# Bias and token sum of the feed-forward output on GpSimd instead of VectorE

## The reference, cut to what matters

```python
t = t + attention(_ln_t(t), ...)      # linear attention, 6 heads
h = relu(_qlinear(_ln_t(t), W1, b1))  # 96 -> 384
t = t + _qlinear(h, W2, b2)           # 384 -> 96
```

## Time and profile before

| | |
|---|---|
| three runs | 4664.05, 4664.84, 4667.7 us; median 4664.84 |
| the profiled execution | 4665.67 us |
| its span, first to last instruction | 4663.9 us |
| busy share of the span | PE 89%, DVE 77%, POOL 53%, ACT 52% |
| TensorE's granted clock, mean | 0.956 of full speed |
| loop blocks | about 3472 to 4465 us of the span |
| last block | about 4465 to 4664 us |

### The profile page before, as it was taken

One profiled execution on the slowest core, in us unless ns is written; L12 is line 12 of the kernel. 1 busy time (PEld: TensorE's weight loads), 2 busy tenths in 40 slices (PEclk: granted clock), 3 DMA queues, 4 the chain that ended last, 5 costly groups with the idle time before them and its releaser, 6 DMA issues. The chain is left out here.

```text
span 4663.9 us, 44769 instructions
## 1 busy us (share of the span) xinstructions
PE 4156.8 (89%) x13922; PEld 1791.2 (38%) x13922; DVE 3569.4 (77%) x4331; ACT 2405.1 (52%) x3937; POOL 2479.7 (53%) x1991
## 2 busy tenths in 40 slices
PE   7999999999999999999999999863989888988964
PEld 2333333333333333333333333221546555655543
DVE  4999999999999999999999999976015415414345
ACT  5666667666666667666666666632012312312223
POOL 4778877888778877888778877761000000000000
PEclk8999999999999999999999999996999999999976
DMA  3444444444444444444444444433010010000000
GB/s 94 131 131 139 135 143 135 137 136 145 135 135 138 133 145 137 136 136 142 136 134 139 137 138 135 127 115 100 12 42 18 18 43 17 18 15 4 18 1 14
DMA packets 135434, 459.67 MB, mean 99 GB/s; under 512 B 20623, under 2 KB 23122, under 8 KB 133662
## 3 DMA queue, kind: packets, MB, share of 16 engines
q1 hardware_dynamic: 135198, 456.82, 32.0%
HBM read 431.28 MB, written 20.97 MB: 97 GB/s over the span
## 5 line engine op out<-in xcount | busy, mean ns | idle before, releaser
L668 POOL TENSOR_TENSOR prod<-states,c_rows 128x512 f32<-128x512 f32 x1536 | 1935.9, 1274 | 591.5 <-DVE states L600 575.7
L600 DVE TENSOR_TENSOR_SCAN states<-decay,carry,bpsum 128x512 f32<-128x512 f32 x1536 | 1937.6, 1262 | 0.0
L357 PE MATMUL ypsum<-prod,identity 128*128 128x512 f32 x3072 | 1587.8, 598 | 0.4 <-POOL prod L668 0.3
L459 ACT ACTIVATE decay<-delta,decay_rate 128x512 f32<-128x512 f32 x1536 | 1078.4, 716 | 722.3 <-DVE states L600 623.6
L587 DVE TENSOR_TENSOR bpsum<-bpsum,dx 128x512 f32<-128x512 f32 x1536 | 1034.8, 674 | 89.9 <-PE bpsum L350 71.7
L350 PE MATMUL bpsum<-b_rows,select 96*128 96x512 bf16 x1536 | 595.4, 388 | 163.7 <-DVE states L600 162.1
L357 PEld LDWEIGHTS ypsum<-prod,identity 128*128 128x128 f32 x3072 | 592.0, 194 | 311.3 <-issue 176.3
L350 PEld LDWEIGHTS bpsum<-b_rows,select 96*128 96x128 bf16 x1536 | 147.9, 96 | 1068.1 <-DVE states L600 666.2
L1073 PE MATMUL convp<-img_hi,w_hi 96*96 96x512 f16 (+1 forms) x1568 | 483.4, 385 | 65.1 <-PEq L1476 49.0
L1434 DVE SCALAR_TENSOR_TENSOR x<-convp,unscale,x_group 96x1024 f32<-96x1024 f32 x16 | 20.4, 1278 | 406.3 <-PE convp L1073 406.3
L1073 PE MATMUL convp<-img_hi,w_lo 128*96 128x512 f16 (+1 forms) x896 | 276.3, 388 | 0.0
(11 more groups left out here) (215 smaller groups left out, 4526.2 us busy)
## 6 DMA issues: line engine op xcount, KB each, us to landing
c_rows<-c_map SPq DMA_DIRECT2D x512, 512.0 KB, 3.7
c_rows<-c_map SPq DMA_DIRECT2D x512, 256.0 KB, 3.9
x_in<-in_x SPq DMA_DIRECT2D x16, 384.0 KB, 6.0
fused_map<-fused SPq DMA_DIRECT2D x16, 384.0 KB, 5.1
work<-fused_map SPq DMA_DIRECT2D x4, 1536.0 KB, 9.8
x<-in_x SPq DMA_DIRECT2D x4, 1536.0 KB, 16.1
x_biased_map<-work SPq DMA_DIRECT2D x4, 1536.0 KB, 7.1
x_group<-x_biased_map SPq DMA_DIRECT2D x16, 384.0 KB, 3.7
```

What stands on the lines that cost most here:

```text
L357: pe.matmul(ypsum[:, group % Y_BANKS, :], identity[:, :], prod[:, n % P_RING, :], start=s == 0, stop=s == STATES - 1).then_inc(summed, 1)
L459: act.activation(decay[:, n % RING, :], delta[k % 2][:, g, :], ACT.Exp, scale=decay_rate[:, ORDER[k][0], g, s:s + 1]).then_inc(decay_ready, 1)
L600: dve.tensor_tensor_scan(states[:, n % H_RING, :], decay[:, n % RING, :], bpsum[:, n % B_BANKS, :], carry[:, at, u:u + 1], ALU.mult, ALU.a ...
L668: pool.tensor_tensor(prod[:, n % P_RING, :], states[:, n % H_RING, :], c_rows[:, n // C_STATES % C_RING, n % C_STATES, :], ALU.mult).then_ ...
```

## The change

DVE's `mlp` loses `add_bias` and both calls of it. A GpSimd program of its own is added to every block with token work. It issues the same two additions, with the same waits and the same semaphores, for the chunks of both layers in order. No other line changes; nothing is computed otherwise.

```diff
                     def mlp(layer):
-                        def add_bias(c):
-                            dve.wait_ge(t_taken, fill_mlp_o(layer, c) + 1)
-                            y = y16[:, c % 2, :, :]
-                            dve.tensor_tensor(y, y, b2[:, layer, :, :], ALU.add).then_inc(y_biased, 1)
-                            dve.wait_ge(y_biased, CHUNKS * layer + c + 1)
-                            tiles = slice(4 * c, 4 * c + 4)
-                            dve.tensor_tensor(t[:, tiles, :], t[:, tiles, :], y, ALU.add).then_inc(t_step, 1)
...
                             to_fp8(c, THIRDS - 1)
-                            if c > 0:
-                                add_bias(c - 1)
-                        add_bias(CHUNKS - 1)
...
+                if tok:
+                    @block.gpsimd
+                    def _(pool):
+                        for layer in range(2):
+                            for c in range(CHUNKS):
+                                pool.wait_ge(t_taken, fill_mlp_o(layer, c) + 1)
+                                y = y16[:, c % 2, :, :]
+                                pool.tensor_tensor(y, y, b2[:, layer, :, :], ALU.add).then_inc(y_biased, 1)
+                                pool.wait_ge(y_biased, CHUNKS * layer + c + 1)
+                                tiles = slice(4 * c, 4 * c + 4)
+                                pool.tensor_tensor(t[:, tiles, :], t[:, tiles, :], y, ALU.add).then_inc(t_step, 1)
```

## The result

The change makes the kernel slower by 0.32%: seven runs have a median of 4681.43 us (4680.52 to 4685.35), against 4666.78 for the kernel before in as many runs (the three of the table above and four more). The ratio is 1.0032, with the interval [1.0022, 1.0042]: 14.65 us. The forecast was 4691 in a range from 4673 to 4714. So the sign and the range were right, and the size was not: 26 us were forecast. (In the times the two lie 9.6 us apart, in the differences 11.4. The rest is chance: the median that the forecast was added to was 1.9 us lower than that of the seven runs.)

The account below looks back on a forecast made before the run. DVE was taken to set the last block's pace, PE's allotted convolution and its exchange with ACT the loop blocks'. The last block's 11 and the loop blocks' 15 make +26 on 4664.84: 4691 us, range 4673 to 4714.

Parts of the forecast that it names:

- Turns between DVE and POOL: Feed-forwards: all six DVE instructions left per chunk take turns with POOL's additions; strictly in turns, 3.8 us a last-block chunk.
- no turns: Whole kernel: POOL and DVE run side by side, gains and losses cancel, net 0, 4665 us; chance 0.12.
- DVE has its way: POOL alone waits, DVE only for an addition already begun: 5 us in loop blocks, 7 in the last, 4677; chance 0.15.
- requests are served as they come: Assumption for the turns: DVE gets in between two POOL instructions, as between two first-block memsets; second memset 4.20 against 4.18 us.
- those with one input, from SBUF to SBUF: The DVE instructions said to wait for POOL's instruction in progress, covering the feed-forward's casts and TENSOR_SCALARs, 0.42 and 0.35 us.
- POOL's price: Each 384-element addition on POOL takes 1.0 us, a pair 2.1 with hand-over, against DVE's 1.19.
- a slow POOL: At 1.27 us an addition, turns take 4.3 us a chunk and delays pile up: 4714 to 4732; chance 0.11.
- bare pair: POOL's last two additions where nothing covers them, as behind layer 1 in loop blocks: 0.9 us more than on DVE.
- Last block, +11 forecast: Last block: seven chunks at 3.4 us and POOL's longer last pair cost 5.5 us per feed-forward, 11 for two.
- I take 3.4, the middle: Last block: us per chunk, chosen between 3.8 strictly in turns and at least 3.1 with fixed parts overlapped.
- Loop blocks, +15 forecast: Loop blocks: 2.1 us behind layer 0 and 3.0 behind layer 1, 5.1 per block, 15 for three; middle chunks free.
- then `y16` of the chunk before (3711.83) brings POOL in twice, a microsecond each, and the last cast ends at 3714.7: Loop blocks, last chunk: two POOL additions delay the last cast from 3712.49 to 3714.7, stalling PE 2.1 us.

Follow-up runs that it names:

- experiment 3: Kernel before, all DVE additions kept, plus the same two additions per chunk on POOL, on tiles nobody reads: 4715.58 us, ratio 1.0107.
- experiment 5: Kernel before plus two POOL memsets of 128x1024 per chunk on a tile of its own, writing only: 4687.16 us, ratio 1.0046.
- experiment 7: Against the kernel before, POOL adds only the first six of eight chunks in loop blocks, DVE the rest: 4666.71 us, ratio 0.9999.

## Why the prediction was right in sign and too high in size

- **Turns between DVE and POOL** were the term that decided, and they are there: experiments 3 and 5 show them without any link of data. The rival "no turns" (4665) fell. The rival "DVE has its way" (4677) is nearer to the time, but not by its mechanism: DVE does wait for POOL, up to 1.4 us for two casts. It did describe a part: POOL also waits through several DVE instructions, as experiment 3 shows, where I had assumed that "requests are served as they come". The sentence "those with one input, from SBUF to SBUF" is too wide: a TENSOR_REDUCE is of that sort and didn't wait (experiment 5).
- **POOL's price.** Taken 1.0 us an addition; where nothing is in its way it takes 0.91, and in the change's mean 1.00 and 0.97. The rival "a slow POOL" fell with it. The bare pair costs 0.8 us more than DVE's, not 0.9. The figure worked out from the Trainium skill's page "GPSIMD Engine Reference", 0.8 for one, is 0.1 too low. Its 2.5 cycles an element stand in the section "Instruction dispatch"; the section that the prediction names has 2.6, which makes an estimate of 0.83.
- **Last block, +11 forecast, +8 measured.** The step that was mis-sized is "I take 3.4, the middle". From the second chunk's start to the last cast's end it is (4565.54 - 4542.88) / 7 = 3.24 us; up to the last chunk it is 3.03, below the bound of 3.1 that I had called the least. The bound assumed that all six DVE instructions and both additions go in turns. In fact in the middle one addition falls into DVE's idle time, where it waits for ACT, every second chunk. Most of what came, 2.6 of 3.9 us in layer 0, came in the last chunk and not spread over seven. Of the 5.5 us per feed-forward, 3.9 and 3.0 came. In layer 0 the seven chunks account for 1.1 of the 1.6 missing (22.7 us instead of 23.8) and the faster first chunk for 0.4, a matter of the clock and not of the reasoning. The tail was forecast at 1.8 + 2.1 = 3.9 us and took 4569.31 - 4565.54 = 3.8. (The high end of this term is twice 4535.07 + 26.6 + 3.9 - 4557.28 = 8.3, so 16.6 and not 16; the range doesn't hang on it.)
- **Loop blocks, +15 forecast, +7 measured.** The failed step is "then `y16` of the chunk before (3711.83) brings POOL in twice, a microsecond each, and the last cast ends at 3714.7". The last chunk doesn't start 0.5 late: 3711.31 is 0.93 behind the 3710.38 of before, and so was the chunk ahead of it (3707.96 to 3707.03), since DVE waited for ACT there anyway. And `y16` is ready at 3712.27 + 0.49 = 3712.76, when DVE has begun the first of its last two casts: POOL gets in once, between them, and its second addition comes behind the last cast. The stall is 0.5 us, not 2.1 (3714.7 - 3712.66 is 2.0), six times. The middle chunks are free, as forecast: experiment 7.
- **Of the sum for the loop blocks**, stalls of 0.5 and 0.5 and a bare pair of 0.8 make 1.8 per block, 5.4 in all. The forecast had 5.1 per block. What is beyond 5.4, some 1.5 to 2 us, goes with the dips of TensorE's clock, which the forecast had no term for. Whether the change causes them is open.
- **What would show it**: the spacing in loop blocks, the wait ahead of L1191 ("near 2.8", it is 2.65), POOL's 1.0 us and its 128 instructions came as said. "The means of L1394 and L1387 rise ... to well over half a microsecond" holds for the casts (602 ns) and not for the TENSOR_SCALARs (390). In the last block's feed-forward of layer 0 it holds for both, 564 and 519 ns over 24 each; in the loop blocks POOL comes in while DVE is at its casts.

## What to carry to other kernels

Work that goes from VectorE to GpSimd isn't all taken off VectorE if what stays there are casts and TENSOR_SCALARs like these, from SBUF to SBUF: they wait for the GpSimd instruction in progress, and the wait is recorded as their own duration (here 71 us of additions left DVE and its busy time fell by 22.5). Here the move was free only where VectorE had idle time and no one asked for the late result, for the first six chunks of the loop blocks, and there it also gained nothing. When such waits are forecast, go through the timeline instruction by instruction and ask which ones are in fact due while the other engine works: the sum by turns gave 26 us where 15 came, because the engines had gaps. And look at the end of each stage first: with nothing behind it to cover a late instruction, the last chunk costs more than those in the middle.

## What was unexpected in the hardware

- An instruction on POOL that is due while DVE has a queue of instructions without gaps can wait through several of them: 2.16 us recorded for 0.91 us of work (experiment 3).
- A DVE addition with two inputs in SBUF waits for a POOL addition (558 to 754 ns in the mean), and not for a POOL memset (558). A TENSOR_REDUCE waits for neither (3.35 us each time).
- On POOL the addition of 128x384 takes the same 0.91 us in 16 bits and in 32 bits. The product of 128x512 takes 1.274 in the mean and 1.252 at least: for a third more elements at least 37% more time. These rows don't show the fixed part that I had carried over from DVE; they are of two operations, so how the time goes with size is not measured.
- TensorE's granted clock falls to its lower level, 1.2 GHz, for some microseconds behind the wait ahead of the output in some loop blocks (0.77 over 7.5 us) and not in others (1.00), with the same kernel and the same 2.65 us of idle time ahead of it. Why it does is open.
